# A 16-batch attention and FFN block on one core: order of the first and the last turns rewritten, two layer norms moved from VectorE to ScalarE, one transpose sent through DRAM

## The chip, the cores and the metric

The kernel runs on one core of a Trainium2 chip. The metric is device time in microseconds; lower is better. PE is TensorE (matmuls), DVE is VectorE, ACT is ScalarE, POOL is GpSimd, SP is SyncE, which here only issues DMAs.

## The reference, cut to what matters

```python
# x: 16 batches of 512 tokens x 256 channels, fp32; 32 heads of 8 channels
qkv = relu(x @ qkv_weight.T);  q, k, v = ...
vk  = einsum(v padded with a column of ones, k)            # per batch and head, 9 x 8
num = vk @ q;  att = num[..., :8] / (num[..., 8:] + 1e-15)
x1  = layernorm(x + att @ proj_weight.T + proj_bias)
h   = silu(x1 @ w_gate.T / 127) * (x1 @ w_up.T / 127)      # 768 hidden channels
out = layernorm(x1 + h @ w_down.T / 127)
```

## The kernel before, in words

One batch of 512 tokens is one unit; a tile is 128 tokens, so a batch has NT = 4 tiles, KC = 2 halves of the channels and NH = 6 blocks of 128 hidden channels. NB = 16. To keep fp32 accuracy on fast matmuls each operand is split in a rounded part (`_hi`, made by ACT) and the rest (`_lo`, made by DVE); a product is then two or three matmuls.

There is no scheduler: each engine has its own instruction list, written by hand, and the lists meet at semaphores. The work is staggered. **Turn i** does the FFN of batch i - 1 and, in turns 1 to 13, projects and normalizes batch i and makes keys, values and queries of batch i + 2. On PE a turn is `gate_up` (6 blocks j of 8 matmuls into the banks gate_ps and up_ps, two of each in alternation), `proj_of(i)`, four `kv_of`, the first tile of `down_of`, `num_of(i + 1)`, `vk_of`, `q_of`, and the other three tiles of `down_of`. Turn 14 has `gate_up(13)`, `proj_of(14)`, `down_of(13)`, transposes of x1 of batch 14 on PE, and `proj_of(15)`. Turn 15 has only `gate_up(14)` and `down_of(14)`. **Turn 16**, the last, has `gate_up(15)` and the last down product, whose four tiles go to four banks of their own, so that each can be normalized as it comes.

Around block j runs a chain: PE ends gate (`gate_mm[j]`), ACT makes `silu`, DVE makes h = up x silu (`h_of`, releases the two banks), ACT rounds it (`h_hi_of`), DVE makes the rest (`h_lo_of`). PE waits for `silu_ok[j-2]` before block j, and for `h_ok[j-2]` after its third matmul; `down_of` waits for `h_ok[5]` first, since it writes gate_ps[1] and up_ps[1], and then for each `h_lo_ok[j]`.

Beside this DVE does the residual additions (`r1_of`, `r2_add`), the statistics (`stats`, `aggregated`, `variance`), the two normalizations (`x1_of`, `out_of`) and the division that gives att; POOL raises the variance to -1/2 (`rstd`) and adds the bias to x (`xb_of`). x1 and att are needed with channels on the partitions. In the steady turns they are turned by DVE in blocks of 32 x 32 (`x1_blocks`, `att_blocks`), written to DRAM and read back with the blocks in place (`x1_there_and_back`, `att_there_and_back` on SP), then split by `..._hi_spread` and `..._lo_spread`. att of batches 0 and 1 are transposed on PE instead (`attT_of`). `out_sb` is the one buffer for finished batches: who writes it first waits until the store of the batch before has landed (`stored`, 16 for each store).

## Time and profile before

| | us |
|---|---|
| median of 3 runs | 504.07 (503.85 to 504.42) |
| the profiled execution, its own time | 504.57 |
| its span in the trace | 502.5 |
| PE busy | 491.4 (98%) |
| DVE busy | 419.7 (84%) |
| ACT busy | 227.7 (45%) |
| POOL busy | 87.3 (17%) |

The span runs from the first to the last event of the trace; 2.07 us of the execution's own time lie around it. PE's busy share counts a matmul that waits in its pipeline as busy, and a slowly clocked one too.

### The profile page before, as it was taken

The page shows a single profiled execution, that of the slowest core. Times are in us where ns is not written, and L with a number is a line of the kernel's source. Part 1 is how long each engine was busy: PE and PEld are TensorE (multiplying, and loading weights), DVE is VectorE, ACT ScalarE, POOL GpSimd, SP SyncE. Part 2 cuts the span into 40 slices and gives each one's busy share as a digit, 9 for nine tenths or more (in the row PEclk, how much of TensorE's full clock was granted, in tenths as well). Part 3 has the DMA queues.
Part 4 walks back from the last instruction along what each step waited for, and adds up shares of the span by engine and source line. Part 5 has one row for each costly group of instructions (what it writes and reads, how often), then busy time and mean ns, then how long its engine had stood idle before and what let it go on. Part 6 is the DMA issues. An engine that isn't in the chain of part 4 may idle for free.

```text
span 502.5 us, 11662 instructions
## 1 busy us (share of the span) xinstructions
PE 491.4 (98%) x4588; PEld 426.6 (85%) x4588; DVE 419.7 (84%) x980; ACT 227.7 (45%) x385; POOL 87.3 (17%) x69
## 2 busy tenths in 40 slices
PE   9999999999999999999999999999999999999796
PEld 5788888888889888888988888888888988798585
DVE  5877878888888888888889798888888888789966
ACT  4667435452453635335362543545245353344333
POOL 1320011311111131112213111131211113013112
PEclk9999999999999999999999999999999999999799
DMA  8421252361705427162442706236170532520402
GB/s 307 157 84 44 85 164 91 122 216 50 254 30 190 144 88 246 42 215 77 167 167 83 247 4 231 103 131 203 57 256 21 192 100 97 196 85 5 158 11 82
DMA packets 48165, 65.33 MB, mean 130 GB/s; under 512 B 2960, under 2 KB 32400, under 8 KB 48144
## 3 DMA queue, kind: packets, MB, share of 16 engines
q1 hardware_dynamic: 48000, 64.77, 37.3%
q8 instruction: 15, 0.25, 0.2%
q10 hardware_dynamic: 144, 0.26, 0.2%
q14 instruction: 6, 0.05, 0.0%
HBM read 35.14 MB, written 23.07 MB: 116 GB/s over the span
## 4 chain that ended last, share of the span: by engine, by line
PE 90%; DVE 7%; issue 1%; ACT 1%; POOL 0%; POOLq 0%
PE up_ps L955 33%; PE gate_ps L955 26%; PE abcd_ps L955 24%; PE abcd_ps L1005 4%; PE gate_ps L983 2%; DVE h L549 1%; DVE st L618 1%; PE gate_ps L1121 1%; DVE r L635 1%; DVE h_lo L542 0%; ACT h_hi L366 0%; DVE attT_lo L542 0%; DVE mv L624 0%; PE abcd_ps L1014 0%; ACT silu L371 0%
## 5 line engine op out<-in xcount | busy, mean ns | idle before, releaser
L295 POOL TENSOR_TENSOR rstd<-ve,minus_half 128x4 f32<-128x4 f32 (+2 forms) x37 | 44.5, 1203 | 324.3 <-DVE ve L630 324.3
L549 DVE SCALAR_TENSOR_TENSOR h<-up_ps,silu 128x512 f32<-128x512 f32 x95 | 65.3, 688 | 29.1 <-PE up_ps L955 17.6
L366 ACT ACTIVATE h_hi<-h 128x512 fp32r<-128x512 f32 (+1 forms) x97 | 60.6, 626 | 57.6 <-DVE h L549 57.1
L371 ACT ACTIVATE silu<-gate_ps 128x512 f32<-128x512 f32 x95 | 55.8, 587 | 61.5 <-PE gate_ps L955 61.5
L955 PE MATMUL up_ps<-x1T_hi,wu_hi 128*128 128x512 f32 x192 | 75.1, 391 | 0.8 <-DVE h L549 0.7
L955 PE MATMUL gate_ps<-x1T_hi,wg_hi 128*128 128x512 f32 x192 | 75.1, 391 | 0.0
L955 PE MATMUL gate_ps<-x1T_lo,wg_hi 128*128 128x512 f32 x192 | 75.0, 391 | 0.0
L955 PE MATMUL up_ps<-x1T_lo,wu_hi 128*128 128x512 f32 x192 | 74.8, 389 | 0.0
L542 DVE TENSOR_TENSOR h_lo<-h,h_hi 128x512 fp32r<-128x512 f32 (+1 forms) x97 | 64.4, 677 | 0.4 <-ACT h_hi L366 0.2
L363 ACT ACTIVATE kv<-abcd_ps 128x512 f32<-128x512 f32 x55 | 32.7, 600 | 61.6 <-PE abcd_ps L955 61.6
L311 POOL TENSOR_TENSOR xb<-x_raw,bias_sb 128x1024 f32<-128x1024 f32 x16 | 38.4, 2402 | 76.7 <-DVE den L572 74.2
L955 PE MATMUL gate_ps<-wd_hi,h_hi 128*128 128x256 f32 x180 | 46.7, 294 | 3.5 <-DVE h L549 3.4
L955 PE MATMUL gate_ps<-wd_hi,h_lo 128*128 128x256 f32 x180 | 46.4, 291 | 0.0
L363 ACT ACTIVATE qT<-up_ps 128x512 f32<-128x512 f32 x27 | 16.2, 599 | 65.8 <-PE up_ps L955 65.7
L618 DVE BATCH_NORM_STATS2 st<-r 128x6 f32<-128x256 f32 x120 | 43.6, 415 | 1.1
L955 PEld LDWEIGHTS up_ps<-x1T_hi,wu_hi 128*128 128x128 f32 x192 | 36.0, 188 | 9.5 <-DVE h L549 1.8
L955 PE MATMUL up_ps<-wd_hi,h_hi 128*128 128x256 f32 x180 | 44.1, 284 | 0.0
L955 PE MATMUL up_ps<-wd_hi,h_lo 128*128 128x256 f32 x180 | 44.0, 284 | 0.0
L955 PE MATMUL abcd_ps<-wkv_hi,xT_lo 128*128 128x512 f32 x110 | 43.2, 393 | 0.0
L955 PE MATMUL abcd_ps<-wkv_hi,xT_hi 128*128 128x512 f32 x110 | 43.0, 391 | 0.0
L955 PEld LDWEIGHTS up_ps<-x1T_lo,wu_hi 128*128 128x128 f32 x192 | 36.1, 188 | 7.4
L955 PE MATMUL abcd_ps<-wkv_lo,xT_hi 128*128 128x512 f32 x110 | 42.3, 389 | 0.0
(179 smaller groups left out, 1045.2 us busy)
## 6 DMA issues: line engine op xcount, KB each, us to landing
x_raw<-x_tok SPq DMA_DIRECT2D x16, 512.0 KB, 5.5
out<-out_sb SPq DMA_DIRECT2D x15, 512.0 KB, 2.7
xT_raw<-x_chan SPq DMA_DIRECT2D x14, 512.0 KB, 6.1
x_way<-wu_raw SPq DMA_DIRECT2D x28, 256.0 KB, 2.1
wd_raw<-x_way SPq DMA_DIRECT2D x28, 256.0 KB, 2.9
...
x<-r SPq DMA_DIRECT2D x13, 512.0 KB, 4.0
```

The source lines that it names most:

```text
L295: nc.gpsimd.tensor_tensor(rs[:, tiles], ve[:, tiles], minus_half[:, tiles], ALU.pow).then_inc(rs_ok, 1)
L311: nc.gpsimd.tensor_tensor(xb[:].rearrange("p (t c) -> p t c", t=NT), x_raw[:].rearrange("p (t c) -> p t c", t=NT), bias_sb[:].unsqueeze(1) ...
L363: nc.scalar.activation(dst, src, ACT.Relu).then_inc(ok, 1)
L366: nc.scalar.activation(dst, src, ACT.Copy).then_inc(ok, 1)
L371: nc.scalar.activation(silu[:, j % 2, :], gate_ps[bank_of(j)][:], ACT.Silu, scale=WSCALE).then_inc(silu_ok[j], 1)
L542: return nc.vector.tensor_tensor(lo, raw, f32(hi), ALU.subtract)
L549: nc.vector.scalar_tensor_tensor(out=h[:, j, :], in0=up_ps[bank_of(j)][:], scalar=WSCALE, in1=silu[:, j % 2, :], op0=ALU.mult, op1=ALU.mul ...
L618: last = nc.vector.bn_stats(st[:, t, :], r[:, t, :])
L635: nc.vector.tensor_tensor(pair(r1, n), (CC, D)[n], xb[:, n * 2 * C:(n + 1) * 2 * C], ALU.add).then_inc(r1_ok[n], 1)
L955: last = mm(dst, lhsT, rhs, start=start and n == 0, stop=stop and n == len(pairs) - 1)
L983: vk_mm_last = mm(bank[g * GC:(g + 1) * GC, k * VW:(k + 1) * VW], kv[:, t, n, 0:GC], kv[:, t, KC * NGC + n, :], start=t == 0, stop=t == NT ...
L1005: last = mm(num_ps[o:o + HP, 2 * k + half, t, :, :].rearrange("p g n -> p (g n)"), q[rows, k, t * P + o:t * P + o + HP], vk[rows, k, :, :] ...
```

## The change

Six things change; nothing is computed in another precision, and no product is added.

- **First turn.** The keys by values of batch 2 (`vk_of(2)`) go right behind num of batch 1, into gate_ps[1], and ahead of q of batch 2, whose second half now uses that bank and waits for `vk_ok`. att of batch 1 is no longer transposed on PE: DVE turns its blocks, and SP sends it through DRAM like the others (so all counts of that path go up by one). The first turn then has the order of the steady ones: six blocks of `gate_up`, then `proj_of(1)`.
- **Turn 13.** num of batch 15 goes ahead of the fourth tile of `down_of(12)`, and DVE makes its reciprocal before the second residual addition.
- **Turn 14.** ACT rounds att of batch 14 a step earlier. DVE's statistics of batch 12 come into this turn, between the h's. Of batch 14, x1 is normalized in front of the small part of att of batch 15, in halves. ACT, not DVE, writes the output of batch 12 (`out_tiles`: Identity with the scale rstd and the bias shift = -mean x rstd, which POOL makes in `shift_of`).
- **Turn 15.** DVE does residual and statistics of batch 15 ahead of the first h, then six h's with two other steps between them. The down product goes to the four banks that the last one uses; tiles 0 and 1 take blocks 0 to 3 first. `h_ok[5]` is still waited for in front of it. The statistics of batch 13 go behind x1T_lo, in the buffers st1, mv1, ve1.
- **Turn 16.** ACT writes the output of batch 13, two tiles behind the first silu, one behind `h_hi` of block 0 and one behind `h_hi` of block 1. `out_of(14)` stays on DVE in front of h of block 3.
- **The end.** Statistics of tiles 0 and 1 of batch 15 are done as one pair.

```diff
...
-                att_there_and_back(i)
+                att_there_and_back(i + 1)
...
+            att_there_and_back(1)
             turn(1)
...
+            def shift_of(count, mv, rs, rs_ok, rs_count, tiles=slice(0, NT)):
+
+                nc.gpsimd.tensor_tensor(neg_mean2[:, tiles], mv[:, tiles, 0], minus_one[:, tiles], ALU.mult).then_inc(neg_mean2_ok, 1)
+                pool.wait_ge(neg_mean2_ok, count)
+                pool.wait_ge(rs_ok, rs_count)
+                nc.gpsimd.tensor_tensor(shift2[:, tiles], neg_mean2[:, tiles], rs[:, tiles], ALU.mult).then_inc(shift2_ok, 1)
...
+            rstd_2(NB - 4)
+            shift_of(1, mv2, rstd2, rstd2_ok, NB - 3)
             for n in range(2):
                 rstd_pair(2, n)
             pool.wait_ge(x1_pair[1], 2)
             xb_of(NB - 1)
-            rstd_2(NB - 4)
 
             rstd_1(NB - 2)
-            rstd_2(NB - 3)
+
+            rstd(NB - 3, ve1, ve2_ok, rstd1, rstd2_ok)
+            shift_of(2, mv1, rstd1, rstd2_ok, NB - 2)
             rstd_2(NB - 2)
-            for t in range(NT):
...
             def first_step():
                 x1_back(r2)
                 q_relu(2, q2_ps, dst=qT_first)
-
-                for j in range(NH):
-                    silu_of(0, j)
-                    if j == 1:
-                        attT_hi_of(1)
-                    h_hi_of(0, j)
-                    if j == 1:
-                        xT_hi_of(3)
+                ffn_step(1)
                 attention_step(1)
...
+            def ffn_step(i):
                 for j in range(NH - 2):
                     silu_of(i - 1, j)
                     if j < NH - 3:
                         h_hi_of(i - 1, j)
+                    if j == 1 and isinstance(i, int) and i == 1:
+                        xT_hi_of(3)
                 attT_hi_spread(i)
                 h_hi_of(i - 1, NH - 3)
                 silu_of(i - 1, 4)
                 silu_of(i - 1, 5)
                 h_hi_of(i - 1, 4, 5)
+
+            def step(i):
+                ffn_step(i)
                 attention_step(i)
+
+            def out_tiles(count, dst, src, rs, tiles):
+                act.wait_ge(shift2_ok, count)
+                for t in tiles:
+                    last = nc.scalar.activation(dst[:, t, :], src[:, t, :], ACT.Identity, bias=shift2[:, t:t + 1],
+                                                scale=rs[:, t:t + 1])
+                return last
...
-                    if j == 1:
+                    if j == 0:
                         attT_hi_spread(i)
                     h_hi_of(i - 1, j)
                 attT_hi_spread(i + 1)
+                act.wait_ge(stored, 16 * (i - 2))
+                out_tiles(1, out_sb, r2, rstd2, range(NT)).then_inc(out_ok, 1)
                 x1T_hi_of(2)
...
+
             silu_of(NB - 1, 0)
+            act.wait_ge(stored, 16 * (NB - 3))
+            out_tiles(2, out_sb, r2_own, rstd1, range(2))
             for j in range(NH - 2):
                 silu_of(NB - 1, j + 1)
                 h_hi_of(NB - 1, j)
+                if j < 2:
+                    last = out_tiles(2, out_sb, r2_own, rstd1, (2 + j,))
+                    if j:
+                        last.then_inc(out_ok, 1)
             h_hi_of(NB - 1, NH - 2)
...
             def first_turn():
-
                 h_of(0, 0, 1)
                 h_lo_of(0, 0)
-                attT_lo_of(1)
-                vk_of(2, CC)
                 h_of(0, 2)
                 h_lo_of(0, 1)
                 h_of(0, 3)
                 xT_lo_of(3)
+                attT_lo_spread(1)
                 h_lo_of(0, 2)
+                h_of(0, 4)
+                h_lo_of(0, 3)
+                h_of(0, 5)
                 r1_of(1)
                 variance_1(1)
-                h_of(0, 4)
-                h_lo_of(0, 3)
+                h_lo_of(0, 4, 5)
                 x1_of(1, r1)
-                h_of(0, 5)
-                h_lo_of(0, 4)
                 x1_blocks(1)
-                h_lo_of(0, 5)
                 dve.wait_ge(x1_turned_back, 1)
...
+            vk_of(2, vk2_ps)
             rden_of(1)
-            att_of(1, turned=True)
+            att_of(1)
+            att_blocks(1)
             first_turn()
             made_ahead(1)
             turn(2)
             with dve.Fori(3, NB - 3) as i:
                 turn(i)
-            turn(NB - 3)
-
-            i = NB - 2
+            i = NB - 3
+            ffn_half(i)
+            attention_half(i)
             rden_of(i + 1)
             att_of(i + 1)
+            vk_of(i + 2, vk_ps)
+            att_blocks(i + 1)
+            x1T_lo_spread(i)
+            r2_add(i - 1, 0)
+
+            rden_of(i + 2)
+            r2_add(i - 1, 1)
...
+            att_of(i + 2)
+
+            i = NB - 2
             h_of(i - 1, 0)
             attT_lo_spread(i)
             h_of(i - 1, 1)
+            stats_2(i - 1)
+            h_of(i - 1, 2)
             att_blocks(i + 1)
-            h_of(i - 1, 2)
-            h_lo_of(i - 1, 0)
             h_of(i - 1, 3)
-            h_lo_of(i - 1, 1)
-            h_lo_of(i - 1, 2)
+            variance_2(i - 2)
+            h_lo_of(i - 1, 0, 1)
             h_of(i - 1, 4)
-            h_lo_of(i - 1, 3)
+            h_lo_of(i - 1, 2, 3)
             h_of(i - 1, 5)
             h_lo_of(i - 1, 4, 5)
             dve.wait_ge(x1_copied, 16 * (i - 1))
             dve.wait_ge(xb_ok, i + 1)
             r1_by_pair(i, 0, 2)
             r1_by_pair(i, 1, 2)
-            attT_lo_spread(i + 1)
             x1_by_pair(att, 0, 2)
+            attT_lo_spread(i + 1, (0,))
             x1_by_pair(att, 1, 2)
+            attT_lo_spread(i + 1, (1,))
 
             r2_add(i - 1, 0, r2_own)
             r2_add(i - 1, 1, r2_own)
             x1T_lo_of(i)
...
             i = NB - 1
             dve.wait_ge(xb_ok, i + 1)
             r1_pair(i, 0)
             stats(st1, r1, 0)
-            h_of(i - 1, 0)
             r1_pair(i, 1)
             stats(st1, r1, 1, st1_ok)
             variance_1(i - 1)
+            h_of(i - 1, 0)
             h_of(i - 1, 1)
-            out_of(i - 3)
+            x1_of(i - 1, r1)
             h_of(i - 1, 2)
-            h_lo_of(i - 1, 0)
-            x1_of(i - 1, r1)
+            x1_blocks(i - 1)
             h_of(i - 1, 3)
-            x1_blocks(i - 1)
-            h_lo_of(i - 1, 1)
+            h_lo_of(i - 1, 0, 1)
             h_of(i - 1, 4)
-            h_lo_of(i - 1, 2)
-            stats_2(i - 1, r2_own)
+            h_lo_of(i - 1, 2, 3)
             h_of(i - 1, 5)
+            h_lo_of(i - 1, 4, 5)
+            x1T_lo_spread(i)
+
+            dve.wait_ge(out_ok, i - 2)
+            stats_2(i - 1, r2_own, st1)
+            variance_2(i - 2, st1, mv1, ve1)
+            dve.wait_ge(x1_turned_back, 2)
+            for n in range(2):
+                dve.wait_ge(down_mm[n], i)
+                for t in (2 * n, 2 * n + 1):
+                    last = nc.vector.scalar_tensor_tensor(out=r2[:, t, :], in0=last_down[t], scalar=WSCALE,
+                                                          in1=x1[:, t, :], op0=ALU.mult, op1=ALU.add)
+                last.then_inc(r2_ok[n], 1)
+
+            i = NB
+            stats_2(i - 1)
+            h_of(i - 1, 0)
             variance_2(i - 2)
-            h_lo_of(i - 1, 3, 4, 5)
-            out_of(i - 2, r2_own)
-            x1T_lo_spread(i)
-            dve.wait_ge(x1_turned_back, 2)
-            r2_add(i - 1, 0)
-            r2_add(i - 1, 1)
-
-            i = NB
-            h_of(i - 1, 0)
-            stats_2(i - 1)
             h_of(i - 1, 1)
-            variance_2(i - 2)
             h_lo_of(i - 1, 0)
             h_of(i - 1, 2)
             h_lo_of(i - 1, 1)
+            dve.wait_ge(out_ok, i - 2)
             out_of(i - 2)
...
+            for n, tiles in enumerate(last_tiles):
+                own_tiles = range(tiles.start, tiles.stop)
+                for t in own_tiles:
+                    dve.wait_ge(down_tile, t + 1)
+                    nc.vector.scalar_tensor_tensor(
+                        out=r2_own[:, t, :], in0=last_down[t], scalar=WSCALE,
+                        in1=r1[:, t, :], op0=ALU.mult, op1=ALU.add).then_inc(r2_tile, 1)
+                for t in own_tiles:
+                    dve.wait_ge(r2_tile, t + 1)
+                    nc.vector.bn_stats(st2[:, t, :], r2_own[:, t, :]).then_inc(st2_tile, 1)
+                dve.wait_ge(st2_tile, tiles.stop)
+                aggregated(st2, mv2, mv2_part, own_tiles)
+                variance(n, mv2, mv2_part, ve2, ve2_part, tiles)
+            dve.wait_ge(rstd2_part, n + 1)
+            normed(out_last, r2_own, mv2, rstd2, out_last_ok, own_tiles)
...
-                down_of(i - 1, (2, 3))
+                down_of(i - 1, (2,))
+                if ahead_of_last_tile:
+                    ahead_of_last_tile()
+                down_of(i - 1, (3,))
...
-            q_of(2, q2_ps)
-            gate_up(0, 0, 1)
-            attT_of(1)
-            vk_of(2)
-            gate_up(0, 2, 3)
-
-            pe.wait_ge(vk_ok, 3)
-            proj_of(1)
-            gate_up(0, 4, 5)
+            vk_of(2, vk2_ps)
+            q_of(2, q2_ps, ahead_of_second=lambda: pe.wait_ge(vk_ok, 3))
+            ffn_half(1)
             attention_half(1, qT_first)
...
+            def num_of_last():
+                num_inputs(NB - 1)
+                pe.wait_ge(att_ok, NB - 1)
+                num_of(NB - 1)
+
+            ffn_half(NB - 3)
+            attention_half(NB - 3, ahead_of_last_tile=num_of_last)
 
             i = NB - 2
-            num_inputs(i + 1)
-            pe.wait_ge(att_ok, i + 1)
-            num_of(i + 1)
...
-            down_of(i - 1)
+
+            pe.wait_ge(h_ok[NH - 1], i)
+            for blocks in (range(4), (4,), (5,)):
+                for t in range(2):
+                    last = down_part(i - 1, t, blocks, last_down[t])
+            last.then_inc(down_mm[0], 1)
+            for t in (2, 3):
+                pe.wait_ge(r1_ok[t - 2], i + 1)
+                last = down_part(i - 1, t, range(NH), last_down[t])
+            last.then_inc(down_mm[1], 1)
...
```

Where the order moves, for the places that the prediction speaks of. DVE in turn 15, from the first residual addition; before (r is r1 of batch 15, then `r<-r,mv,rstd` is x1 of 14, `out_sb` the output of 12):

```order
L635 TENSOR_TENSOR r<-abcd_ps,xb 128x512
L618 BN_STATS st<-r 128x6 x2
L549 SCALAR_TENSOR_TENSOR h<-up_ps,silu 128x512
L635 TENSOR_TENSOR r<-abcd_ps,xb 128x512
L618 BN_STATS st<-r 128x6 x2
L791 COPY st_seen<-st 128x1
L624 BN_AGGR mv<-st 128x2 x4
L630 TENSOR_SCALAR ve<-mv 128x4
L549 SCALAR_TENSOR_TENSOR h<-up_ps,silu 128x512
L671 TENSOR_SCALAR out_sb<-r,mv,rstd 128x256 x4
L549 SCALAR_TENSOR_TENSOR h<-up_ps,silu 128x512
L542 TENSOR_TENSOR h_lo<-h,h_hi 128x512
```

and now:

```order
L656 TENSOR_TENSOR r<-abcd_ps,xb 128x512
L639 BN_STATS st<-r 128x6 x2
L656 TENSOR_TENSOR r<-abcd_ps,xb 128x512
L639 BN_STATS st<-r 128x6 x2
L812 COPY st_seen<-st 128x1
L645 BN_AGGR mv<-st 128x2 x4
L651 TENSOR_SCALAR ve<-mv 128x4
L570 SCALAR_TENSOR_TENSOR h<-up_ps,silu 128x512 x2
L692 TENSOR_SCALAR r<-r,mv,rstd 128x256 x4
L570 SCALAR_TENSOR_TENSOR h<-up_ps,silu 128x512
L760 STREAM_TRANSPOSE wu_raw<-r 128x4x4x32 x2
L570 SCALAR_TENSOR_TENSOR h<-up_ps,silu 128x512
```

The output of batch 12 and one statistics group are gone from here, and the first h stands behind the whole residual of batch 15 and no longer in its middle.

ACT in turn 16, from its first silu, with waits; before:

```order
L371 ACTIVATE silu<-gate_ps 128x512 [waits gate_mm0]
L371 ACTIVATE silu<-gate_ps 128x512 [waits gate_mm1]
L366 ACTIVATE h_hi<-h 128x512 [waits h_ok0]
L371 ACTIVATE silu<-gate_ps 128x512 [waits gate_mm2]
L366 ACTIVATE h_hi<-h 128x512 [waits h_ok1]
```

and now:

```order
L380 ACTIVATE silu<-gate_ps 128x512 [waits gate_mm0]
L502 ACTIVATE out_sb<-r_own,shift,rstd 128x256 [waits shift2_ok,stored]
L502 ACTIVATE out_sb<-r_own,shift,rstd 128x256
L380 ACTIVATE silu<-gate_ps 128x512 [waits gate_mm1]
L375 ACTIVATE h_hi<-h 128x512 [waits h_ok0]
L502 ACTIVATE out_sb<-r_own,shift,rstd 128x256 [waits shift2_ok]
L380 ACTIVATE silu<-gate_ps 128x512 [waits gate_mm2]
L375 ACTIVATE h_hi<-h 128x512 [waits h_ok1]
L502 ACTIVATE out_sb<-r_own,shift,rstd 128x256 [waits shift2_ok]
```

The output of batch 13 is done in four pieces; the last, which releases the store, stands behind `h_hi` of block 1.

DVE in turn 16, around the output of batch 14, with waits; before:

```order
L549 SCALAR_TENSOR_TENSOR h<-up_ps,silu 128x512 [waits up_mm2,silu_ok2]
L542 TENSOR_TENSOR h_lo<-h,h_hi 128x512 [waits h_hi_ok1]
L671 TENSOR_SCALAR out_sb<-r,mv,rstd 128x256 [waits rstd2_ok,stored]
L671 TENSOR_SCALAR out_sb<-r,mv,rstd 128x256 x3
L549 SCALAR_TENSOR_TENSOR h<-up_ps,silu 128x512 [waits up_mm3,silu_ok3]
```

and now:

```order
L570 SCALAR_TENSOR_TENSOR h<-up_ps,silu 128x512 [waits up_mm2,silu_ok2]
L563 TENSOR_TENSOR h_lo<-h,h_hi 128x512 [waits h_hi_ok1]
L692 TENSOR_SCALAR out_sb<-r,mv,rstd 128x256 [waits rstd2_ok,stored,out_ok]
L692 TENSOR_SCALAR out_sb<-r,mv,rstd 128x256 x3
L570 SCALAR_TENSOR_TENSOR h<-up_ps,silu 128x512 [waits up_mm3,silu_ok3]
```

The rows are the same but for a wait on `out_ok` at the output of batch 14; its wait on `stored` is the old one, but the store that it waits for now comes out of ACT's pieces above.

## Rows read from the trace of the kernel before

**Rows 1.** The page, part 1: busy us, share of span and instructions

```profile
PE 491.4 (98%) x4588; PEld 426.6 (85%) x4588; DVE 419.7 (84%) x980; ACT 227.7 (45%) x385; POOL 87.3 (17%) x69
```

**Rows 2.** The waits of PE: us in total, times, longest us

```profile
PE gate_ps L955 <- DVE h L549: 3.4, 1, 3.4
...
PE up_ps L955 <- DVE h L549: 0.7, 1, 0.7
PE gate_ps L1093 <- DVE att L678: 0.6, 1, 0.6
```

**Rows 3.** Windows: busy of each engine, granted clock, DMA share, GB/s

```profile
468.30:471.30 3.00, 0.16 (x1) 0.00 (x0) 3.00 (x8) 1.11 (x2) 0.00 (x0) 0.99 0.54 197
471.30:478.00 6.70, 6.08 (x27) 5.79 (x28) 5.40 (x16) 1.90 (x3) 1.38 (x1) 0.50 0.43 148
```

**Rows 4.** Timeline of PE, turns 13 to 16: start, duration, what, idle before

```profile
431.23 0.50 PE L955 MATMUL gate_ps<-x1T_hi,wg_hi 128*128 128x512 f32 x1
...
443.39 0.28 PE L955 MATMUL abcd_ps<-wp_hi,attT_lo 128*128 128x256 f32 x1
...
452.92 0.44 PE L1093 MATMUL gate_ps<-consts,att 128*128 128x128 f32 x2 [0.63 <-DVE att L678]
...
456.95 0.40 PE L955 MATMUL gate_ps<-x1T_hi,wg_hi 128*128 128x512 f32 x1
...
480.67 0.40 PE L955 MATMUL gate_ps<-x1T_hi,wg_hi 128*128 128x512 f32 x1
...
490.45 0.39 PE L955 MATMUL up_ps<-x1T_hi,wu_hi 128*128 128x512 f32 x1
...
491.58 0.28 PE L955 MATMUL abcd_ps<-wd_hi,h_hi 128*128 128x256 f32 x1
...
497.21 0.28 PE L955 MATMUL abcd_ps<-wd_hi,h_lo 128*128 128x256 f32 x1
```

**Rows 5.** Timeline of DVE and ACT, turn 14: blocks 2 and 3

```profile
439.48 0.69 DVE L549 SCALAR_TENSOR_TENSOR h<-up_ps,silu 128x512 f32<-128x512 f32 x1
...
440.20 0.63 ACT L366 ACTIVATE h_hi<-h 128x512 fp32r<-128x512 f32 x1 [0.76 <-DVE h L549]
...
441.35 0.69 DVE L549 SCALAR_TENSOR_TENSOR h<-up_ps,silu 128x512 f32<-128x512 f32 x1 [0.59 <-ACT silu L371]
```

**Rows 6.** Timeline of DVE, turn 15: first residual addition, and h after the statistics

```profile
457.82 0.69 DVE L635 TENSOR_TENSOR r<-abcd_ps,xb 128x512 f32<-128x512 f32 x1
...
461.87 0.69 DVE L549 SCALAR_TENSOR_TENSOR h<-up_ps,silu 128x512 f32<-128x512 f32 x1
```

**Rows 7.** Timeline of ACT and DVE, turn 16; the page, part 6

```profile
486.15 0.62 ACT L366 ACTIVATE h_hi<-h 128x512 fp32r<-128x512 f32 x1
...
496.79 0.60 ACT L531 ACTIVATE out_last<-r_own,shift,rstd 128x256 f32<-128x256 f32 x1 [3.49 <-POOL shift L357]
...
487.62 1.38 DVE L671 TENSOR_SCALAR out_sb<-r,mv,rstd 128x256 f32<-128x256 f32 x4
...
out<-out_sb SPq DMA_DIRECT2D x15, 512.0 KB, 2.7
```

**Rows 8.** Timeline of DVE, tail: first and last residual tile of batch 15

```profile
494.41 0.42 DVE L935 SCALAR_TENSOR_TENSOR r_own<-abcd_ps,r 128x256 f32<-128x256 f32 x1 [0.65 <-PE abcd_ps L955]
...
498.02 0.41 DVE L935 SCALAR_TENSOR_TENSOR r_own<-abcd_ps,r 128x256 f32<-128x256 f32 x1
```

**Rows 9.** Timeline, first turn, then a steady one

```profile
44.25 1.03 PE L1014 MATMUL abcd_ps<-consts,att 128*128 128x128 f32 x8
...
46.37 1.06 ACT L366 ACTIVATE xT_hi<-xT_raw 128x1024 fp32r<-128x1024 f32 x1
...
50.62 1.22 DVE L542 TENSOR_TENSOR xT_lo<-xT_raw,xT_hi 128x1024 fp32r<-128x1024 f32 x1
...
400.17 0.40 PE L955 MATMUL gate_ps<-x1T_hi,wg_hi 128*128 128x512 f32 x1
...
408.68 1.28 DVE L542 TENSOR_TENSOR attT_lo<-wkv_raw,attT_hi 128x512 fp32r<-128x512 f32 x2
```

More of the change, by code:

```diff
@@ L529, in _ @@
             for t in range(NT - 1):
-                act.wait_ge(shift2_tile, t + 1)
-                nc.scalar.activation(out_last[:, t, :], r2_own[:, t, :], ACT.Identity, bias=shift2[:, t:t + 1],
-                                     scale=rstd2[:, t:t + 1]).then_inc(out_tile, 1)
+                out_tiles(3 + t // 2, out_last, r2_own, rstd2, (t,)).then_inc(out_tile, 1)
         @block.vector
@@ L956, in add_up, with q_of @@
                 return last
-            def q_of(b, banks=(A, B), xT_hi=xT_hi, xT_lo=xT_lo):
+            def q_of(b, banks=(A, B), xT_hi=xT_hi, xT_lo=xT_lo, ahead_of_second=None):
                 for k in range(KC):
+                    if k and ahead_of_second:
+                        ahead_of_second()
                     o = slice(k * P, (k + 1) * P)
```

64 lines of the change are left out of this document (24 added, 40 removed).

## Prediction

> **What bounds the kernel now.** I read the page first, for who is busy: PE, 98% [rows 1]. So time can be won only where PE waits, runs at a lower clock, or does work that can go. The waits of PE are few: 3.4 us on h in one place, 0.7 us on h in another, 0.6 us on a normalized tile, all of them on DVE [rows 2]. The windows then show what the longest wait does. In the 3 us after block 5 of turn 15 PE is busy for 0.16 us, and in the 6.7 us that follow it works at a granted clock of 0.50, the lower of its two levels, 1.2 GHz [rows 3]. Last, the timeline of PE gives the length of each stretch at the end [rows 4]. A `gate_up` without a wait takes 491.58 - 480.67 = 10.91 us, which is 1.82 a block. A matmul of 256 columns takes (497.21 - 491.58) / 47 = 0.120 us, so a down product (48 of them) 5.75 us.
>
> I call G the start of `gate_up` in a turn. Against these lengths the end of the program loses:
>
> - turn 14, `gate_up`: 443.39 - 431.23 = 12.16, so 1.25 us lost (the wait on h, the restart behind it);
> - turn 14, `proj` and `down`, 72 matmuls of 0.120 = 8.64, to the transposes: 452.92 - 443.39 = 9.53, so 0.89 lost;
> - turn 15: 480.67 - 456.95 = 23.72 against 10.91 + 5.75 = 16.66, so 7.06 lost: the wait, and about 3.35 for 6.7 us at half the clock.
>
> The steady turns have no wait of PE, and the change leaves them as they are.
>
> **Turn 14, -2.2 us.** DVE's queue here holds the reciprocal and att of batch 15, h, attT_lo, h. num of batch 15 now runs one down tile (12 x 0.120 = 1.44 us) earlier and half of att's work gets done while PE still multiplies; ACT rounds attT ahead of h_hi of block 0. Counted along the durations of DVE, h of block 1 starts some 4.1 us behind G. PE asks for it in block 3, at 3 x 1.82 + 0.7 = 6.2. The statistics of batch 12 (1.4 us, moved here from behind x1T) fit in the slack. I take the whole 1.25 us. Of the 0.89 I take 0.85: attT_lo of batch 15 no longer stands in front of x1, and everything is a microsecond earlier against PE's own work; the first transpose then finds x1 ready. Behind them `proj(15)` needs the second half of attT_lo just when PE gets there: 0.1 us gained, or 0.3 lost. Together 2.2 us, between 1.6 and 2.3. ACT's four output pieces lie in a stretch where it has nothing to do.
>
> **Turn 15, -4.95 us.** Two things decide when h of block 5 is there, and PE still waits for it in front of the down product. The first is the pace. In this turn ACT rounds h of block j before it makes silu of j + 1, so a block can't take less than h, h_hi, silu, h: 441.35 - 439.48 = 1.87 us [rows 5], a little more than PE's 1.82. Now all that stands between two h's (x1 in four pieces, the block transposes, pairs of h_lo; 1.2 to 1.3 us each) fits in that cycle; before, the output of batch 12, x1, the transposes and the statistics did not, and it ran behind. The second is the start. Residual, statistics and variance of batch 15 take 461.87 - 457.82 = 4.05 us with one h of 0.60 between them [rows 6], so 3.45 alone. They start when x1T_lo of batch 14 is done, which I put at G - 0.65 (between -1.05 and -0.3). So h of block 0 starts at G + 2.8, h of block 5 at 2.8 + 5 x 1.87 = G + 12.15, and ends at G + 12.85. PE has done its blocks at G + 10.91. It still waits, 1.95 us, and loses 0.15 on the restart. Of the 7.06 that leaves 7.06 - 2.1 = 4.95, if the clock stays up. Waits of 0.6 and 0.7 us left it up, 3.4 us took it down [rows 2, 3]; 1.95 lies between, nearer to the short ones. The lower bound of this term is therefore 4.95 - 3.1 = 1.85.
>
> **Turn 16, +2.1 us: a new wait.** This is the term that speaks against the change. `out_sb` is one buffer. `out_of(14)` on DVE must wait until the store of batch 13 has landed, and that store now waits for ACT's last piece. h_hi of block 1 starts at 486.15 - 480.67 = G + 5.48 [rows 4, 7]; the last piece starts 0.53 later (ACT's own pace in rows 5, 0.63 less a short overlap) and takes 0.60, as the same operation does in the tail [rows 7]. So the store is issued at G + 6.65, and with 2.7 us to landing [rows 7] it is there at G + 9.35. DVE stands at this output from 487.62 - 480.67 = G + 6.95. Behind it in DVE's queue is h of block 3: 1.29 for the four tiles, then h at G + 10.65, done at G + 11.35. PE wants it at the fourth matmul of block 5, 490.45 - 480.67 = G + 9.78 [rows 4]. That is a wait of 1.55 us, 0.2 for the restart, and about 0.35 more at the down product, since h_lo of block 4 and h of block 5 come 0.6 later against PE than they do now. Sum 2.1. Less than 1.2 would need a store of 1.8 us; at 3.3 it is 2.7.
>
> The Trainium skill ("DMA: Bandwidth & Descriptors", section "Anatomy of one DMA") gives a DMA (fitted on GpSimd's path) about 2.0 us of fixed cost, mostly the write receipt, plus its bytes at 436 GB/s. For 512 KB that is an estimate of 3.2 us, half a microsecond over the measured 2.7; by it turn 16 would cost 2.6 and the sum below be 5.0. I keep the row of this kernel. The same skill ("ScalarE: Activation LUTs", section "What ACT_TABLE_LOAD costs") gives 186 ns plus 0.833 ns an element plus 93 ns for each pointer operand, 0.585 us for 256 elements with a scale and a bias; the trace's 0.60 agrees.
>
> **The tail, -0.35 us.** The four tiles now keep DVE busy without a pause, 498.02 - 494.41 = 3.61 us for three, 1.20 each [rows 8]. Tiles 0 and 1 as a pair spare one set of waits, 0.4. PE's last matmul starts at 497.21 and takes 0.28 more [rows 4], so the last tile can't start before 497.53, and 0.5 is the upper bound; 0 if POOL gets in the way. I take 0.35.
>
> **The first turn, -0.1 us.** The eight transposes of att go, 0.96 us of PE [rows 9], and 0.15 for one restart. But att of batch 1 now has to be ready where the steady turns have it. There attT_lo is done at 408.68 + 1.28 - 400.17 = G + 9.8 [rows 9], 1.1 before PE ends its blocks. The trip through DRAM is no part of that: by the durations of DVE its block transposes end about G + 1.4, there and back are two transfers, each of half the bytes of a store that takes 2.7 [rows 7], so att is back near G + 7, and ACT comes to it at G + 8.7. But the first turn has the first xT_hi on ACT (1.06 us) and xT_lo on DVE (1.22) ahead of attT_lo [rows 9], which the steady ones do elsewhere. Both together move it to G + 11.8, so PE waits 0.9 and restarts. Gain 1.1, loss 1.0. Bounds: -1.1 if all is hidden, +0.4 if the delay on ACT comes in full.
>
> **The sum.** 2.2 + 4.95 - 2.1 + 0.35 + 0.1 = 5.5 us. The profiled execution took 504.57 us, its span 502.5; it would take 499.1. It lies 0.5 above the median of the runs, 504.07, so the forecast for that is 504.07 - 5.5 = 498.6.
>
> **The rivals.**
>
> - *The clock falls in turn 15 after all.* A wait of 1.95 us in front of the down product, on top of what a wait of 3.4 us did. Price as in the trace, 6.7 us at 0.50 with the restart, 3.1 us: 501.7. For it: [rows 3], where the clock fell though PE had been busy for 0.16 of the 3 us. Against: the wait is little more than half as long. 14%.
> - *No new wait in turn 16.* If the store is early or DVE late enough, turn 16 stays at its 16.5 us, and the time is 496.5. Against it: the order itself; the store can't be issued before silu of block 2 and h_hi of block 1. 9%.
> - *More is hidden, or less, in turns 1, 14 and 15*, at the far ends of the bounds above: 497.0 or 500.4. 11%.
> - *Slower.* Waits of 1 to 2 us are enough to bring the clock down, at 3.1 us each. There are three: attT_lo in the first turn, h in turn 15, h in turn 16. Two of them give 504.8, all three 507.9. It decides from the point at which a wait of about 1 us suffices; waits of 0.6 and 0.7 us in turn 14 did not [rows 2]. 4% for three, 2% for two.
>
> **How the numbers follow.** The forecast has 60%, and its own range is 497.3 to 499.9. The whole range, 496.4 to 501.8, leaves out the slower cases and thin ends, and takes in the clock's fall. A measurement of this kernel tells 0.2%, 1.0 us, from no change. Faster by more than that is every case down to 501.8: 0.94. Within 0.2%: 0.02 (two falls of the clock). Slower: 0.04.
>
> **What would show it.** Right: PE's longest waits are about 1.5 us in turn 16 and 2 us in turn 15, both on h, one below 1 us in the first turn at `proj_of(1)`, none in turn 14; the granted clock is 1.00 after turn 15's wait; DVE idles for 2.4 us in front of `out_of(14)`, and the store of batch 13 is what ends it; `gate_up(14)` to `gate_up(15)` takes 18.8 us and not 23.7. Wrong: a clock of 0.50 anywhere; a wait at the transposes of batch 14 or at `proj(15)`; a first turn that loses more than 1 us at attT_lo, with the DRAM path as its releaser.

## The result, and the profile after

The changed kernel takes 500.37 us (median, 499.88 to 500.74) against 504.12 (503.85 to 504.42): ratio 0.9925, 95% interval 0.9910 to 0.9941, 3.75 us faster. The forecast was 5.5 us faster, 498.6. The profiled execution took 500.56 us with a span of 498.5, against 504.57 and 502.5; so the two spans differ by 4.0 us, the medians by 3.75.

Page, part 1, of the changed kernel, beside [rows 1]:

```profile
PE 487.9 (98%) x4580; PEld 423.3 (85%) x4580; DVE 418.3 (84%) x963; ACT 231.8 (46%) x393; POOL 88.1 (18%) x70
```

The waits of PE (total, times, longest us), beside [rows 2]:

```profile
PE abcd_ps L991 <- DVE h L570: 1.7, 1, 1.7
PE up_ps L991 <- DVE h L570: 1.4, 1, 1.4
...
PE abcd_ps L991 <- DVE attT_lo L563: 0.7, 1, 0.7
PE gate_ps L991 <- ACT silu L380: 0.4, 1, 0.4
PE gate_ps L1131 <- DVE att L699: 0.2, 1, 0.2
```

The 3.4 us wait of turn 15 is now 1.7. The wait of 1.4 is the new one of turn 16, that of 0.7 stands at `proj_of(1)` in the first turn. A wait in turn 14, which was to go, is still there: 0.4 us, on silu. Windows of turn 15's wait and of the down product behind it, beside [rows 3] (the granted clock is the third number from the end):

```profile
466.90:469.10 2.20, 0.47 (x3) 0.07 (x1) 2.20 (x5) 1.20 (x3) 0.00 (x0) 1.00 0.78 236
469.10:474.90 5.80, 5.80 (x49) 5.80 (x50) 4.99 (x15) 1.59 (x3) 1.24 (x3) 1.00 0.02 5
```

The clock is 1.00 where it was 0.50. The timeline of PE, beside [rows 4]:

```profile
430.88 0.40 PE L991 MATMUL gate_ps<-x1T_hi,wg_hi 128*128 128x512 f32 x1
...
442.71 0.28 PE L991 MATMUL abcd_ps<-wp_hi,attT_lo 128*128 128x256 f32 x1
...
451.85 0.27 PE L1131 MATMUL gate_ps<-consts,att 128*128 128x128 f32 x1
...
456.24 0.40 PE L991 MATMUL gate_ps<-x1T_hi,wg_hi 128*128 128x512 f32 x1
...
469.03 0.38 PE L991 MATMUL abcd_ps<-wd_hi,h_hi 128*128 128x256 f32 x1 [1.73 <-DVE h L570]
...
474.88 0.40 PE L991 MATMUL gate_ps<-x1T_hi,wg_hi 128*128 128x512 f32 x1
...
493.71 0.28 PE L991 MATMUL abcd_ps<-wd_hi,h_lo 128*128 128x256 f32 x1
```

Subtracting neighbours here and in [rows 4] splits the 4.0 us between the two spans:

| stretch of PE | before | after | measured | forecast |
|---|---|---|---|---|
| to the start of turn 14, whose `gate_up` is that of batch 13 | 431.23 | 430.88 | -0.35 | -0.1 |
| turn 14: `gate_up` | 12.16 | 11.83 | -0.33 | -1.25 |
| turn 14: `proj`, `down`, to the transposes | 9.53 | 9.14 | -0.39 | -0.85 |
| turn 14: transposes, `proj(15)` | 4.03 | 4.39 | +0.36 | -0.1 |
| turn 15 | 23.72 | 18.64 | -5.08 | -4.95 |
| turn 16, to the last matmul | 16.54 | 18.83 | +2.29 | +2.1 |
| last matmul to the end of the span | 5.29 | 4.79 | -0.50 | -0.35 |

Outside turn 14 every row is within 0.25 us of its forecast. Turn 14 should have given 2.2 us and gave 0.36. The timeline of ACT in turn 14 shows who is late (the bracket is the idle time before, and what ended it):

```profile
432.24 0.60 ACT L380 ACTIVATE silu<-gate_ps 128x512 f32<-128x512 f32 x1 [5.18 <-PE gate_ps L991]
433.99 0.63 ACT L375 ACTIVATE attT_hi<-wkv_raw 128x512 fp32r<-128x512 f32 x1 [1.16 <-DMA wkv_raw<-att_way]
435.19 0.63 ACT L375 ACTIVATE attT_hi<-wkv_raw 128x512 fp32r<-128x512 f32 x1 [0.57 <-DMA wkv_raw<-att_way]
```

ACT waits for att of batch 14 to come back from DRAM. Everything behind it in ACT's queue, h_hi and silu of block 1, moves back with it. SP's timeline shows that the trip back begins late: 5.00 us lie between the issue of the write and that of the read. In the ten steady turns it is 2.9.

```profile
426.18 1.27 SPq L215 DMA_DIRECT2D att_way<-wg_raw  x2
431.18 0.92 SPq L221 DMA_DIRECT2D wkv_raw<-att_way  x2
```

The view of the DMA queues for 426 to 432 us has a second queue, with one packet, and the write takes 5.0 us to land:

```profile
q1 hardware_dynamic: 432, 1.05, 46.1%
q8 instruction: 1, 0.02, 1.0%
...
att_way<-wg_raw SPq DMA_DIRECT2D x2, 256.0 KB, 5.0
```

The packets themselves, from the records of the trace (start, what, how long):

```
to 429.42   the write's 2048 B packets, on 16 DMA engines, 0.08 to 0.15 us each
429.14      q8, instruction fetch, 16384 B, 0.94 us
430.07      2048 B, 0.23 us
430.29      4 B (a semaphore increment of the first half)
430.30      8 packets of 2048 B, one after the other, to 431.18
431.18      4 B (a semaphore increment of the second half)
```

From 429.42 to 431.18 nothing moves but what looks like one engine's remaining share, begun as the fetch ends. Of the 16 increments of the first half's semaphore 15 are there by 429.13, the last (the packet of 430.29) is booked at 431.17, and SP issues the read at 431.18. The Trainium skill ("DMA: Bandwidth & Descriptors", section "Why a DMA increments its semaphore by 16 and not by 1") says that the engines finish on their own and that only the full 16 means landed; the trace agrees, with 2.04 us between the 15th and the 16th.

That gave the theory, **A**: PE's turn 13 now stands behind its loop (`Fori(2, NB - 3)` where the kernel before has `NB - 2`, a line that the diff ahead of the prediction does not show), so PE has new code to fetch in it, and one fetch of 16 KB falls on the write. In the kernel before, no fetch of 16 KB came between 102.0 and 435.8 us. The page counts 18 such packets on q8, and 15 before; that they are PE's is read from this: they move and change in number with edits to PE's code. Rivals: **B**, VectorE's new order costs the time in turn 14; **C**, chance; **D**, being behind the loop, not the fetch.

### The profile page after: what moved, and what is told of

It is laid out like the page before. It is cut to its first block, busy times and chain, and to the rows that moved or that the text cites. A ratio compares the mean times of both kernels' runs of the same rounds, so it can differ in the third digit from the quotient of the medians.

```text
span 498.5 us, 11660 instructions
## 1 busy us (share of the span) xinstructions
PE 487.9 (98%) x4580; PEld 423.3 (85%) x4580; DVE 418.3 (84%) x963; ACT 231.8 (46%) x393; POOL 88.1 (18%) x70
## 4 chain that ended last, share of the span: by engine, by line
PE 81%; DVE 8%; issue 4%; DMA 3%; ACT 2%; POOL 1%; SPq 0%; POOLq 0%; DVEq 0%
PE up_ps L991 29%; PE abcd_ps L991 23%; PE gate_ps L991 22%; PE abcd_ps L1043 3%; DVE h L570 2%; PE gate_ps L1021 2%; DVE st L639 1%; DVE h_lo L563 1%; DMA att_way<-wg_raw 1%; PE gate_ps L1162 1%; POOL rstd L298 1%; ACT h_hi L375 1%; DMA wkv_raw<-att_way 1%; DMA wd_raw<-x_way 1%; ACT silu L380 1%
## 5 line engine op out<-in xcount | busy, mean ns | idle before, releaser
L991 PEld LDWEIGHTS gate_ps<-x1T_hi,wg_hi 128*128 128x128 f32 x192 | 36.1, 188 | 7.7 <-ACT silu L380 0.8
L991 PEld LDWEIGHTS gate_ps<-x1T_lo,wg_hi 128*128 128x128 f32 x192 | 36.1, 188 | 7.1 <-issue 0.2
L991 PE MATMUL gate_ps<-wd_hi,h_hi 128*128 128x256 f32 x168 | 41.5, 283 | 0.2 <-issue 0.2
L991 PE MATMUL gate_ps<-wd_hi,h_lo 128*128 128x256 f32 x168 | 41.4, 283 | 0.0
```

What stands on the lines that cost most here:

```text
L991: last = mm(dst, lhsT, rhs, start=start and n == 0, stop=stop and n == len(pairs) - 1)
```

## The experiments

They ran in three sets, each beside the kernel before, which took 504.39 us (loop_longer, skipped_code, own_buffer, no_h5_wait), 503.99 (changed_again, all_three, longer_wait, first_turn_undone) and 504.20 (shorter_code, attT_lo_ahead). The ratios are against that neighbour. In all of them the two numbers that the theory turns on can be read off the trace:

| kernel | fetch near the write | att write issued | read issued | behind it | median us |
|---|---|---|---|---|---|
| changed (first profile) | 429.14 | 426.18 | 431.18 | 5.00 | 500.37 |
| changed_again | 428.44 | 426.04 | 430.90 | 4.86 | 500.39 |
| own_buffer | 428.78 | 425.90 | 430.81 | 4.91 | 497.86 |
| no_h5_wait | 428.75 | 426.35 | 431.20 | 4.85 | 499.67 |
| longer_wait | 428.66 | 426.26 | 431.11 | 4.85 | 504.09 |
| first_turn_undone | 428.89 | 426.03 | 430.93 | 4.90 | 500.81 |
| attT_lo_ahead | 428.85 | 425.98 | 430.89 | 4.91 | 500.80 |
| skipped_code | 426.97 | 427.37 | 430.92 | 3.55 | 501.03 |
| shorter_code | 430.74 | 427.02 | 430.09 | 3.07 | 499.58 |
| loop_longer | none to 437.22 | 425.87 | 428.84 | 2.97 | 499.24 |
| all_three | none to 437.20 | 425.71 | 428.68 | 2.97 | 495.40 |

The traces hold a second test that no edit was made for. In turn 2, the first pass through PE's loop, a 16 KB fetch comes at 101.1 to 102.0 us in every kernel, the one before included, and falls between the write of att (98.2 to 99.4) and its read. There the read stands 3.4 to 5.0 us behind the write, in loop_longer too, whose turn 13 is clean:

```profile
98.97 1.19 SPq L215 DMA_DIRECT2D att_way<-wg_raw  x2
103.86 0.93 SPq L221 DMA_DIRECT2D wkv_raw<-att_way  x2
```

In the ten turns behind it, where no fetch comes, it is 2.9 to 3.0 us in all twelve profiles. In turn 2 PE has no wait either way; that trip has slack there.

**loop_longer**: one part undone (VectorE's second residual addition of that turn goes ahead of the reciprocal to suit).

```diff
+            r2_add(i - 1, 1)
             rden_of(i + 2)
-            r2_add(i - 1, 1)
...
-            with pe.Fori(2, NB - 3) as i:
+            with pe.Fori(2, NB - 2) as i:
...
-            ffn_half(NB - 3)
-            attention_half(NB - 3, ahead_of_last_tile=num_of_last)
+            num_inputs(NB - 1)
+            pe.wait_ge(att_ok, NB - 1)
+            num_of(NB - 1)
```

> The changed kernel with one part undone: TensorE's turn 13 stands in its loop again, and num of batch 15 follows the loop (with VectorE's second r2 ahead of rden of batch 15 to suit). Theory A, late write: the 16 KB instruction fetch that came at 429.14 us in turn 13 of the changed kernel stands before the last 2 KB packets of the att write on one DMA engine, so the write lands at 431.17 and the turned read is issued at 431.18, not 2.9 us behind the write as in the steady turns. With turn 13 in the loop no fetch falls there: the read is issued 2.8 to 3.2 us behind the write, block 1 of turn 14 no longer waits for it, turn 14 ends 1.0 to 1.8 us earlier, and the time is 498.6 to 499.6 us. Theory B, the order of VectorE's work in turn 14 (the h cycle, blocks, statistics) is what costs the missing 1.85 us: the time stays at 500.1 to 500.7 us.

Measured: 499.24 us (ratio 0.9909, 0.9893 to 0.9924). No fetch in turn 13, 2.97 us, and ACT no longer waits for the DMA:

```profile
432.21 0.60 ACT L380 ACTIVATE silu<-gate_ps 128x512 f32<-128x512 f32 x1 [5.19 <-PE gate_ps L991]
432.70 1.14 ACT L375 ACTIVATE attT_hi<-wkv_raw 128x512 fp32r<-128x512 f32 x2
434.25 0.63 ACT L375 ACTIVATE h_hi<-h 128x512 fp32r<-128x512 f32 x1 [0.40 <-DVE h L570]
```

PE's timeline of turn 14:

```profile
430.75 0.50 PE L991 MATMUL gate_ps<-x1T_hi,wg_hi 128*128 128x512 f32 x1
...
441.76 0.28 PE L991 MATMUL abcd_ps<-wp_hi,attT_lo 128*128 128x256 f32 x1
...
450.38 0.27 PE L1131 MATMUL gate_ps<-consts,att 128*128 128x128 f32 x1
...
454.77 0.40 PE L991 MATMUL gate_ps<-x1T_hi,wg_hi 128*128 128x512 f32 x1
```

`gate_up` takes 11.01 us (forecast 12.16 - 1.25 = 10.91), the way to the transposes 8.62 (forecast 9.53 - 0.85 = 8.68). With the read on time the two terms come out as forecast, against B. The last stretch stays at 4.39. This edit also puts num of batch 15 back behind the fourth down tile, so that part of the change was not needed for the gain.

**skipped_code**: 70 matmuls ahead of turn 13 and 58 ahead of turn 14's down product, inside branches that are not taken.

```diff
+            with pe.If_ne(flag, 0):
+                for n in range(70):
+                    mm(gate_ps[0][:], wg_lo[:, 0, 0:P], x1T_hi[:, 0, :], start=True, stop=True)
             ffn_half(NB - 3)
```

> The changed kernel with 70 matmuls more in TensorE's code ahead of turn 13 and 58 ahead of the down product of turn 14, all inside branches that are skipped, so nothing more is computed; the instruction fetches move to other times. Theory A, late write: the fetch of 429.14 us comes some 3 to 4 us earlier, ahead of the att write's packets (426.6 to 429.4), the read is issued about 2.9 us behind the write, and the time is 498.6 to 499.8 us; if the fetch falls on the write all the same, the read stays late and the time at 500.4. Theory B, VectorE's order in turn 14: no change, 500.1 to 500.7 us. Rival C, the skipped branches and one fetch more cost time of their own: up to 0.3 us over the changed kernel.

Measured: 501.03 us (0.9939, 0.9925 to 0.9953), a miss on the time. The fetch moved by 2 us, not 4, and the write came later, so it fell on the write's start; the read came 3.55 behind. And a cost appeared that no theory had, in the middle of turn 13's small `vk` matmuls. The timeline of PE:

```profile
421.71 0.30 PE L1021 MATMUL gate_ps<-kv 128*32 128x36 f32 x12
424.07 0.25 PE L1021 MATMUL gate_ps<-kv 128*32 128x36 f32 x2 [2.06 <-issue]
```

PE stands for 2.06 us, and nothing that the profile shows holds it; the fetch before it started at 421.57. That PE waited for its own code there is argued, not shown. Behind the stand the granted clock is down (window, third number from the end):

```profile
424.54:427.96 3.42, 3.42 (x9) 2.68 (x9) 1.34 (x3) 0.60 (x1) 0.00 (x0) 0.50 0.33 98
```

The products for q are spaced 0.43 us in it and not 0.23, 1.6 us more in all. The stand and the lower clock make up the 3.46 us by which turn 14 starts later than in the changed kernel (434.34 against 430.88), and with them the miss on the time. VectorE had this time as a lead into turn 14, which then took 457.76 - 434.34 = 23.42 us, what the forecast gave it (25.72 - 2.2 = 23.52).

**shorter_code**: turn 13 stays behind the loop; its `gate_up` alone loses the branch with the products of the weights' low parts (not taken with these weights).

```diff
-                    with pe.If_ne(flag, 0):
-                        add_up(gate, gate_lo, start=False, stop=False)
-                        add_up(up, up_lo, start=False, stop=False)
+                    if lo_too:
+                        with pe.If_ne(flag, 0):
+                            add_up(gate, gate_lo, start=False, stop=False)
+                            add_up(up, up_lo, start=False, stop=False)
...
-            ffn_half(NB - 3)
+            ffn_half(NB - 3, lo_too=False)
```

> The changed kernel, turn 13 still behind TensorE's loop, but in that turn alone the branch with the products of the low parts of wg and wu (skipped with these weights, as the flag is zero) is left out of the gate and up blocks, so the same matmuls run and the code of the turn is some 108 instructions shorter. Theory A, the fetch itself and not the turn's place behind the loop delays the att write: the fetch of 428.4 to 429.1 us comes at 432 us or later, off the write; the read is issued 2.9 to 3.0 us behind the write, turn 14 is 1.1 to 1.5 us shorter and the time is 499.0 to 499.5 us. Rival, something else in having the turn behind the loop delays it: the read stays 4.8 to 5.0 us behind the write and the time at 500.1 to 500.6 us.

Measured: 499.58 us (0.9912, 0.9895 to 0.9929); the read 3.07 us behind, turn 14 455.24 - 430.93 = 24.31 us against 25.36. The fetch came at 430.74, sooner than I expected, but after the write; it lay beside the read instead, which then took 3.4 us to land and not 3.0, and 0.3 us of loop_longer's gain are missing (454.77 - 430.75 = 24.02 us there). With the turn still behind the loop, D falls.

**changed_again**: the changed kernel once more.

> The changed kernel itself, unchanged, beside the other kernels of this set on one chip. Theory A, the late write of turn 13 comes from the program: the read of att is again issued 4.8 to 5.0 us behind the write (5.00, 4.91 and 4.85 us in the three kernels with the same TensorE code so far), and the time is 500.0 to 500.8 us. Rival, chance: the read comes 2.9 us behind the write and turn 14 is 1.4 us shorter, 499.0 us.

Measured: 500.39 us (0.9937, 0.9918 to 0.9955), 4.86 us. With seven profiles of the same PE code in turn 13 all between 4.85 and 5.00, C falls. In all seven 15 of the 16 increments are there in time and the last comes 1.86 to 2.04 us behind them. What the late read costs varies more: turn 14 takes 25.03 to 25.67 us in the seven, and 24.02 and 24.04 in loop_longer and all_three.

**own_buffer**: batch 14's output goes through a free buffer.

```diff
-            store(NB - 2)
+            sp.wait_ge(out_ok, NB - 1)
+            sp.dma_start(out[NB - 2], xb[:]).then_inc(stored, 16)
...
-            out_of(i - 2)
+            dve.wait_ge(rstd2_ok, i - 1)
+            normed(xb[:].rearrange("p (t c) -> p t c", c=C), r2, mv2, rstd2, out_ok)
```

> The changed kernel, but the output of batch 14 in turn 16 is written to the buffer xb, which is free by then, and stored from there, so VectorE does not wait for the store of batch 13's output. Theory A, the store wait is what turn 16 pays: the 2.30 us wait of the out pieces (481.91 to 484.21 us) is gone, h of block 3 comes some 2.2 us earlier, turn 16 is about 1.4 to 2.2 us shorter, and the time is 498.2 to 499.0 us. Rival, another chain (ScalarE's silu and h_hi, or the matmuls themselves) is as late: under 0.6 us is gained, 499.8 us or more.

Measured: 497.86 us (0.9877, 0.9862 to 0.9892). DVE's timeline, first of the changed kernel, then of this one:

```profile
481.23 0.68 DVE L563 TENSOR_TENSOR h_lo<-h,h_hi 128x512 fp32r<-128x512 f32 x1
484.21 1.38 DVE L692 TENSOR_SCALAR out_sb<-r,mv,rstd 128x256 f32<-128x256 f32 x4 [2.30 <-issue]
485.51 0.68 DVE L570 SCALAR_TENSOR_TENSOR h<-up_ps,silu 128x512 f32<-128x512 f32 x1
```

```profile
480.58 0.68 DVE L564 TENSOR_TENSOR h_lo<-h,h_hi 128x512 fp32r<-128x512 f32 x1
481.18 1.38 DVE L693 TENSOR_SCALAR xb<-r,mv,rstd 128x256 f32<-128x256 f32 x4
482.47 0.68 DVE L571 SCALAR_TENSOR_TENSOR h<-up_ps,silu 128x512 f32<-128x512 f32 x1
```

The 2.30 us are booked as "issue", since the profile names no instruction that ends them; the store did. Without it turn 16 takes 490.77 - 474.23 = 16.54 us, to the hundredth what it took before.

**no_h5_wait**: PE's wait for the last h ahead of turn 15's down product is left out; its banks are free, and each h_lo is still waited for.

```diff
-            pe.wait_ge(h_ok[NH - 1], i)
             for blocks in (range(4), (4,), (5,)):
```

> The changed kernel without TensorE's wait for h of the last block ahead of the down product of batch 14 in turn 15 (its banks are free anyway, and each block's h_lo is still waited for). Theory A: the 1.73 us wait at 467.15 to 469.03 us is nearly gone, 16 matmuls of blocks 0 to 3 run in it, then the products of blocks 4 and 5 wait for their h_lo (469.5 and 470.2 us); the down product ends 1.2 to 1.5 us earlier, and the time is 498.8 to 499.3 us. Rival: turn 16 then starts against VectorE, which has x1T_lo, statistics and r2 still to do, or against the store wait, and gives it back: 500.0 us or more.

Measured: 499.67 us (0.9911, 0.9897 to 0.9924), 0.7 gained where 1.2 to 1.5 were expected: turn 15 takes 473.99 - 456.07 = 17.92 against 18.64. The 16 matmuls of blocks 0 to 3 that are ready (two tiles, 8 each) run in the wait, then PE waits again for h_lo of blocks 4 and 5 (0.5 us in all). Turn 16 stays at 18.83: nothing is given back.

**longer_wait**: six pieces more of VectorE work between h of blocks 3 and 4 of turn 15.

```diff
+            for n, t in enumerate((0, 1, 2, 3, 0, 1)):
+                junk = out_last[:, t, :] if n < 4 else x_raw[:, t * C:(t + 1) * C]
+                nc.vector.tensor_scalar(junk, r1[:, t, :], mv1[:, t, 0:1], rstd1[:, t:t + 1], ALU.subtract, ALU.mult)
             h_of(i - 1, 4)
```

> The changed kernel with six pieces of VectorE work more (the form of out's pieces, into tiles that nobody reads then) between h of block 3 and h of block 4 of turn 15, some 2.0 us by the 1.38 us of four; so TensorE's wait ahead of the down product grows from 1.73 to about 3.7 us, more than the stretch of 3.0 us at a busy share of .16 in the kernel before. Theory A, that wait is what brought the clock down to .50 in the kernel before, and its absence is what turn 15 gained beside the work: the granted clock falls behind the wait, the down product of 48 matmuls takes 8 to 11.5 us in place of 5.85, and the time is 504 to 507.5 us. Rival B, the fall came from something else in that turn: the down product keeps 5.85 us and the time is 502.0 to 502.6 us.

Measured: 504.09 us (1.0008, 0.9997 to 1.0018), 3.7 over the changed kernel. Windows of the wait and of the down product:

```profile
467.05:470.67 3.62, 0.03 (x2) 0.00 (x1) 3.62 (x9) 1.14 (x3) 0.00 (x0) 1.00 0.47 139
470.67:478.03 7.36, 7.36 (x49) 7.36 (x50) 5.06 (x15) 1.65 (x3) 1.38 (x3) 0.77 0.02 3
```

Behind a wait of 3.62 us the clock is down, behind one of 1.73 it is not. It costs 7.36 - 5.85 = 1.5 us on top of the wait, half of what [rows 3] led me to price (3.1): here the first 15 matmuls are spaced 0.21 us, the rest 0.12. The down product took less than the 8 to 11.5 us that I expected, and the time is at the lower end. Skipped_code has a case between the two: its stand of 2.06 us, behind 126 short matmuls, brought the clock down as well.

**first_turn_undone**: the first turn of the kernel before (att of batch 1 turned by PE) in the changed kernel.

```diff
-            vk_of(2, vk2_ps)
-            q_of(2, q2_ps, ahead_of_second=lambda: pe.wait_ge(vk_ok, 3))
-            ffn_half(1)
+            q_of(2, q2_ps)
+            gate_up(0, 0, 1)
+            attT_of(1)
+            vk_of(2)
+            gate_up(0, 2, 3)
...
+            pe.wait_ge(vk_ok, 3)
+            proj_of(1)
+            gate_up(0, 4, 5)
```

> The changed kernel with the first turn of the kernel before: att of batch 1 turned by TensorE's transposes (8 matmuls and 4 rounds from PSUM) and vk of batch 2 behind them. Forecast's theory: the first turn's rewriting gained 0.1 us, so the time is 500.4 to 500.7 us; the trace's marks say 0.3 us up to the first block of turn 2 (102.03 us before, 101.74 after), so 500.5 to 500.8 us. Rival, the new way costs or brings more than the marks of one pair of profiles show (0.7 us wait for attT_lo in the new way): outside 500.2 to 501.0 us.

Measured: 500.81 us (0.9944, 0.9927 to 0.9962). The runs alone can't tell this from 500.39; PE's marks can: from num of batch 1 to the first kv of batch 3 it takes 55.76 - 36.12 = 19.64 us, in changed_again 55.46 - 36.00 = 19.46. The first pair of profiles says the same, 56.21 - 36.58 = 19.63 before and 55.92 - 36.47 = 19.45 after. The rest of this profile's time is no effect of the first turn: its turn 16 takes 19.24 us where every other kernel with the store's wait has 18.81 to 18.84. An 8 KB instruction fetch, on q14, comes at 483.40, on the store of batch 13:

```profile
q14 instruction: 1, 0.01, 0.4%
...
out<-out_sb SPq DMA_DIRECT2D x1, 512.0 KB, 3.0
```

That store lands 3.0 us behind its issue where the changed kernel's takes 2.6, and DVE's idle time grows from 2.30 to 2.70. No run moved this fetch by itself, so the cause is argued.

**attT_lo_ahead**: one piece of VectorE's order undone.

```diff
-            x1_by_pair(att, 0, 2)
-            attT_lo_spread(i + 1, (0,))
-            x1_by_pair(att, 1, 2)
-            attT_lo_spread(i + 1, (1,))
+            attT_lo_spread(i + 1)
+            x1_by_pair(att, 0, 2)
+            x1_by_pair(att, 1, 2)
```

> The changed kernel with one part undone: in turn 14 both halves of attT_lo of batch 15 stand ahead of the x1 pieces again, as in the kernel before (450.83 and 452.04 us there), not the first half between them and the second behind. Theory A: the order moved the transposes ahead by one half (0.6 us) and made proj of batch 15 wait for the second half behind them, so of that 0.6 us only about 0.25 are kept; undone, the transposes start 0.6 us later, proj follows them by 1.1 us in place of 1.44, and the time is 0.2 to 0.3 us more than the changed kernel's 500.39, 500.6 to 500.7 us. Rival, r1 and the first h of turn 15 hang on the transposes and the x1T pieces, and all 0.6 us are lost: 501.0 us.

Measured: 500.80 us (0.9933, 0.9919 to 0.9948), above the 500.6 to 500.7 of the expectation, though by the ratios to their neighbours the runs can't tell it from the changed kernel (0.9937). By PE's marks the transposes start 9.90 us behind `proj(14)` and not 9.14, and the last stretch takes 4.03 us, as before, and not 4.39. So of 0.76 us gained ahead of the transposes 0.36 are lost behind them, where `proj(15)` waits for the second half.

**all_three**: loop_longer and own_buffer, and the down product of turn 15 begun with blocks 0 to 3 of all four tiles.

```diff
-            pe.wait_ge(h_ok[NH - 1], i)
-            for blocks in (range(4), (4,), (5,)):
+            for t in range(NT):
+                if t >= 2:
+                    pe.wait_ge(r1_ok[t - 2], i + 1)
+                down_part(i - 1, t, range(4), last_down[t])
+            for blocks in ((4,), (5,)):
```

> The changed kernel with the three edits together: turn 13 in TensorE's loop, batch 14's output through xb without the wait for the store, and the down product of turn 15 begun with blocks 0 to 3 of all four tiles without the wait for h of the last block (32 matmuls, 3.8 us of work for a wait of 1.7 us and the two waits for h_lo behind it). Theory A, the three costs lie one behind the other on the path: 1.1 us (499.24 against 500.37) and 2.3 us (497.86) and, with four tiles ahead where the trial with two gave 0.7 us, 1.6 to 1.9 us, so 495.2 to 495.8 us. Rival, VectorE is the bound of turns 15 and 16 and the down product's gain is given back ahead of turn 16 (r2 of batch 14 comes no sooner than x1T_lo and the statistics allow): 496.5 to 497.0 us.

Measured: 495.40 us, ratio 0.9831 (0.9815 to 0.9846): 8.6 us under the kernel before and 5.0 under the changed one, and the fastest kernel of the study. Turn 15 takes 472.02 - 454.79 = 17.23 us, turn 16 16.54. After 400 us one wait of PE is left:

```profile
PE gate_ps L1133 <- DVE att L700: 0.2, 1, 0.2
```

## Why the prediction was right, and where it was off

The time, 500.37, lies in the range, 1.8 us above the forecast; "faster" was right. Step by step:

- **Turn 14, -2.2: mis-sized, measured -0.36.** The sum counted the durations of PE, ACT and DVE, and took "ACT rounds attT ahead of h_hi of block 0" as free. It said of the steady turns that "the change leaves them as they are", but turn 13 leaves PE's loop, and it didn't ask what that adds: code to fetch by DMA. The late write costs 25.36 - 24.02 = 1.34 us of the missing 1.84 in this profile (1.0 to 1.65 over the seven). The other 0.5 is the sentence "Behind them `proj(15)` needs the second half of attT_lo just when PE gets there: 0.1 us gained, or 0.3 lost": its worse side came true, +0.35 to +0.39 in every profile with this order but skipped_code's, where VectorE had its lead.
- **Turn 15, -4.95: right, -5.08.** h of block 0 starts at 458.89, which is G + 2.65 (forecast 2.8), that of block 5 at 468.29, G + 12.05 (12.15), so the cycle of 1.87 us sets the pace. PE waits 1.73 us (1.95). The clock stays up, and that was partly luck: the forecast judged the wait by those of 0.6, 0.7 and 3.4 us, and the longest wait for h that left it up is one of 1.8 us (first_turn_undone, turn 16), the next longer one is 3.43. Skipped_code's stand of 2.06 us, in another place, is near the forecast's 1.95 and did bring the clock down. longer_wait shows a wait for h at which it falls, for half of the rival's price of 3.1.
- **Turn 16, +2.1: right, +2.29.** ACT's last piece starts at 480.88, G + 6.00 (6.01), the store is issued at 481.50, G + 6.62 (6.65), DVE's output at G + 9.33 (9.35), h of block 3 at G + 10.63 (10.65). own_buffer shows that this wait is the whole of the term. The estimate of 3.2 us for a 512 KB store that came from the Trainium skill ("DMA: Bandwidth & Descriptors", section "Anatomy of one DMA"), from a fit on GpSimd's path, does not hold for these stores, which SP issues: they land in 2.7 us.
- **The tail, -0.35: -0.50, the upper bound**; POOL did not get in the way. **The first turn, -0.1: -0.18**, by both pairs of profiles; the wait at `proj_of(1)` is 0.71 us where 0.9 was worked out. The 0.35 us in the table's first row are this 0.18 and 0.17 that lie elsewhere, 0.11 of it ahead of num of batch 1, where two profiles of the same kernel differ by 0.47 (36.47 and 36.00).
- "Right: none in turn 14" was the sign to look for, and it failed: 0.4 us on silu. The wrong signs that were named (clock, transposes, `proj(15)`) did not include a late DMA in turn 14, though its releaser would have named it at once.

Theory A is shown: the fetch's place was moved in three ways, and the read followed each time (in skipped_code only in part, 3.55 us, since the fetch met the write's start), and turn 2 shows the same in all twelve profiles. That the fetch and the write's last packets share one DMA engine is read from their order in time; the trace doesn't name the engine of a packet.
